# Output weights of a state space scan: four raw slots instead of two, and the across term scaled in the buffer of exp(cs)

## What is computed

```python
proj = hidden_states @ in_proj_w.T                 # gate, x/B/C, dt
hBC  = silu(conv(hBC) + conv_b)                    # 4 taps along time
A_cumsum = cumsum(-exp(A_log) * dt)                # "cs" of each head, within a chunk
Y_diag = einsum('bclsh,bcshp->bclhp', (C @ B.T) * exp(segment_sum(A)), x * dt)
Y_off  = einsum('bclhn,bchpn->bclhp', C, states) * exp(A_cumsum)[..., None]
y = Y_diag + Y_off + D * x
y = y * rsqrt(mean(y**2) + EPS) * norm_w
out = (y * silu(gate)) @ out_proj_w.T
```

## Time and profile before

| | us |
|---|---|
| median of 3 runs | 1904.71 |
| lowest, highest | 1900.41, 1908.31 |
| the profiled execution | 1903.86 |
| its span, first to last instruction | 1901.8 |

### The profile page before, as it was taken

How to read it: one execution, slowest core, us unless ns; L and a number is a source line. 1 busy time by engine, 2 the same in 40 slices (tenths; PEclk the granted TensorE clock), 3 DMA queues, 4 the chain that set the end, 5 groups by cost and what they waited for, 6 DMA issues and landing times. The chain is left out here.

```text
span 1901.8 us, 28929 instructions
## 1 busy us (share of the span) xinstructions
PE 1717.6 (90%) x9420; PEld 1395.2 (73%) x9420; DVE 1209.1 (64%) x1848; ACT 1264.8 (67%) x2162; POOL 738.2 (39%) x785
## 2 busy tenths in 40 slices
PE   5997739999999998999899989998999899999839
PEld 4876527787878787878787878787878787878627
DVE  4665555666666676657665766666766575767763
ACT  3331214986788778867786778677867786788711
POOL 2553012353345434543453345344434344444530
PEclk9998769999999999999999999999999999999969
DMA  4310114323232323332333232322332332232221
GB/s 149 105 62 1 61 58 121 100 85 107 78 102 88 105 84 102 94 93 84 98 91 100 80 99 86 102 79 92 101 96 77 98 98 87 85 100 80 67 70 44
DMA packets 99607, 166.93 MB, mean 88 GB/s; under 512 B 11729, under 2 KB 50129, under 8 KB 98033
## 3 DMA queue, kind: packets, MB, share of 16 engines
q1 hardware_dynamic: 99440, 164.84, 27.3%
HBM read 158.51 MB, written 6.29 MB: 87 GB/s over the span
## 5 line engine op out<-in xcount | busy, mean ns | idle before, releaser
L217 PE MATMUL bank<-xh,w_h 128*128 128x512 f32 x1152 | 463.7, 403 | 12.1 <-SPq L1083 11.3
L218 PE MATMUL bank<-xl,w_h 128*128 128x512 f32 x1152 | 451.2, 392 | 5.3 <-issue 5.3
L219 PE MATMUL bank<-xh,w_l 128*128 128x512 f32 x1152 | 451.5, 392 | 0.0
L1186 POOL TENSOR_TENSOR m_z_l<-m_zg,m_z_h 128x512 fp32r<-128x512 f32 x128 | 189.2, 1478 | 561.5 <-ACT m_z_h L1288 561.5
L1240 ACT ACTIVATE m_mt<-m_mt,m_unit 128x128 f32<-128x128 f32 x1024 | 312.1, 390 | 0.0
L1165 POOL TENSOR_TENSOR w_l<-w_raw,w_h 128x512 fp32r<-128x512 f32 x142 | 184.4, 1298 | 300.3 <-ACT w_h L1207 300.3
L1319 DVE TENSOR_TENSOR acc<-acc,bank 128x512 f32<-128x512 f32 x128 | 87.9, 687 | 301.9 <-PE bank L219 286.1
L217 PEld LDWEIGHTS bank<-xh,w_h 128*128 128x128 f32 x1152 | 217.5, 189 | 65.9 <-SPq L1083 11.5
L217 PE MATMUL bank<-m_wo_h,m_z_h 128*128 128x512 f32 x512 | 211.3, 413 | 55.0 <-DVE m_wo_l L1337 50.0
L1309 DVE SCALAR_TENSOR_TENSOR m_xc<-bank,m_par_conv,m_xc 128x1020 f32<-128x1020 f32 (+2 forms) x192 | 244.6, 1274 | 21.2 <-ACT m_xc L1219 16.6
L219 PEld LDWEIGHTS bank<-xh,w_l 128*128 128x128 f32 x1152 | 217.1, 188 | 52.7 <-issue 6.3
(11 more groups left out here) (238 smaller groups left out, 2804.7 us busy)
## 6 DMA issues: line engine op xcount, KB each, us to landing
m_mt<-ncs_rows SPq DMA_DIRECT2D x128, 512.0 KB, 3.9
w_raw<-w_in SPq DMA_DIRECT2D x144, 256.0 KB, 3.2
m_e<-ecs_rows SPq DMA_DIRECT2D x128, 128.0 KB, 3.5
m_wo_raw<-w_out_in SPq DMA_DIRECT2D x64, 256.0 KB, 2.7
a_wo_raw<-wo_in SPq DMA_DIRECT2D x8, 1024.0 KB, 4.7
x<-x_in SPq DMA_DIRECT2D x8, 256.0 KB, 4.6
a_wq_raw<-wq_in SPq DMA_DIRECT2D x8, 256.0 KB, 3.4
e_wb_raw<-f_base SPq DMA_DIRECT2D x2, 1024.0 KB, 7.9
```

The source lines that it names most:

```text
L217: nc.tensor.matmul(out, ah, bh, start=first, stop=False)
L218: nc.tensor.matmul(out, ah, bl, start=False, stop=False)
L219: return nc.tensor.matmul(out, al, bh, start=False, stop=last)
L1186: nc.gpsimd.tensor_tensor(z_l[:, s % 2, :, :], zg[:], f(z_h[:, s % 2, :, :]), ALU.subtract).then_inc(zl_ready, 1)
```

## The change

- WO_BUFS goes from 2 to CT = 4: each of a half's four tiles has its own raw slot.
- SP no longer loads tiles 2 and 3 of the present half in step t = 1. In t = 2 it loads all four of the next half, each after the low part that frees its slot. At the start four tiles are loaded ahead, not two.
- ScalarE, step t = 1: first the eviction and `w_high` of the step, then the four high parts, then `decay(s+2)`.
- VectorE, step t = 1: the four low parts in one row, behind `times_dt` and ahead of off, y and zg.
- The buffer `off` goes. The across term is written over the slot of `e` it was scaled with, and y adds that. SP's reload of the slot waits for `y_ready` of the step instead of `off_ready`.

```diff
-W_BUFS, WO_BUFS, ROW_BUFS = 3, 2, 4
+W_BUFS, WO_BUFS, ROW_BUFS = 3, CT, 4
...
-        off = sb("off", [P, CT, P])
...
                 def step(g, s, kind):
                     half, t = divmod(s, NT)
-                    if own(kind) and t == 1:
+                    if own(kind) and t == 2 and (half == 0 or kind != "last"):
                         for k in range(WO_BUFS):
                             sp.wait_ge(wo_split, wo_at(g, half, k))
-                            load_wo(g, half, k + WO_BUFS)
-                    if own(kind) and t == 2 and (half == 0 or kind != "last"):
-                        for k in range(WO_BUFS):
-                            sp.wait_ge(wo_split, wo_at(g, half, k + WO_BUFS))
                             load_wo(g + half, 1 - half, k)
...
                     if s % 2 == 1 and own(kind) and ahead(kind, s + 4):
-                        sp.wait_ge(off_ready, pair(g, s))
+                        sp.wait_ge(y_ready, at(g, s))
                         load_e(g, s + 4)
...
                     half, t = divmod(s, NT)
-                    if own(kind) and t == 1:
-                        for k in range(WO_BUFS):
-                            wo_high(g, half, k)
                     for m in EARLY[s]:
                         if has_tile(kind, m):
                             evict(g, m)
                             if has_tile(kind, m + 2):
                                 w_high(g, m + 2)
+                    if own(kind) and t == 1:
+                        for k in range(CT):
+                            wo_high(g, half, k)
                     if ahead(kind, s + 2):
                         decay(g, s + 2)
...
-                    if own(kind) and t == 1:
-                        for k in range(WO_BUFS, CT):
-                            wo_high(g, half, k)
...
                     if own(kind) and t == 1:
-                        for k in range(WO_BUFS):
+                        for k in range(CT):
                             wo_low(g, half, k)
...
-                            nc.vector.tensor_tensor(off[:], bank[:, 5, :].rearrange("p (c l) -> p c l", c=CT),
-                                                    e[:, s // 2 % 2, :, :], ALU.mult).then_inc(off_ready, 1)
+                            off = e[:, s // 2 % 2, :, :]
+                            nc.vector.tensor_tensor(off, bank[:, 5, :].rearrange("p (c l) -> p c l", c=CT), off,
+                                                    ALU.mult).then_inc(off_ready, 1)
...
-                            last = nc.vector.tensor_tensor(y[:], y[:], off[:], ALU.add)
+                            last = nc.vector.tensor_tensor(y[:], y[:], off, ALU.add)
...
-                        if t == 1:
-                            for k in range(WO_BUFS, CT):
-                                wo_low(g, half, k)
```

## The result

| | before | changed |
|---|---|---|
| median of the runs | 1904.32 us (4 runs) | 1828.84 us (4 runs) |
| lowest, highest | 1900.41, 1908.31 | 1827.55, 1829.94 |
| the profiled execution, its span | 1903.86, 1901.8 | 1827.55, 1825.8 |
| mean granted clock of TensorE | 0.954 | 0.966 |

The ratio is 0.9601, 95% interval 0.9581 to 0.9620. Forecast were 1833 us, range 1826 to 1860.

What follows compares the result with a forecast made beforehand. The prediction took TensorE's matmuls to bound the kernel. Terms of 44.6 + 23.6 + 3.0 = 71.2 us off the profiled 1903.86 gave 1832.7, and 0.85 to the median gave 1833 us, range 1826 to 1860.

Steps and rivals of the forecast that it cites:

- 15 waits on the lows: Step 1 of the 15 half groups with a projection: TensorE's wait ahead of add_up goes entirely, 44.6 us.
- clock behind them: TensorE's lowered clock in the 12 us after those waits returns to full: 23.6 us, bounds 0 and 25.2.
- last half of the last group: Step 9, no projection as cover: wait falls from 5.45 to some 2.3 us, gain 3.0 us, bounds 0 and 7.0.
- Highs in one row: ACT, step 1: eviction and w_high fit its idle time, then four highs end at 919.9, ahead of the decay.
- Lows in one row: DVE, step 1: four lows end at about 921.3, TensorE asks at 925.09; cover 3.8 us, so the wait goes.
- rival A: DVE's row of lows is stretched, 15 us given back: 1848 us, or 1872 with the cold clock too; chance 0.12.
- Slots and loads: Two more slots, SP's loads moved to step 2, seven steps ahead of use: cost 0.
- off in the buffer of exp(cs): Same instruction with another destination, slot reload some 2 us later under 44 us of cover: cost 0.
- B: Rival: TensorE's cold stretches stay or come elsewhere, 1856 us; chance 0.11.
- C: Rival: another wait stood behind the low parts' wait all the time, so no gain, 1904 us; chance 0.05.
- D: Rival: four highs ahead of the decay delay decay, mask and diag two steps later; slower, about 1924 us; chance 0.02.

Runs made afterwards that it cites:

- e1: The kernel before with four raw slots and the changed kernel's loads, highs and lows in their old places; 1906.86 us, ratio 1.0006.
- e2: The kernel before with four slots and the four highs in one row behind eviction and w_high, lows still split; 1834.95 us, ratio 0.9637.
- e3: The kernel before with four slots and the four lows in one row ahead of off, y and zg, highs still split; 1903.74 us, ratio 0.9989.
- e6: The changed kernel with the four highs ahead of the eviction and w_high instead of behind them; 1829.50 us, ratio 0.9598 to the kernel before.
- e5: The kernel before with twelve unused matmuls on TensorE ahead of the wait for the lows in add_up; 1877.24 us, ratio 0.9859.
- e4: The kernel before with only the across term scaled in the slot of exp(cs), no buffer off, reload waiting for y_ready; 1902.07 us, ratio 0.9978.
- c: The changed kernel itself, run once more as a yardstick; 1828.25 us, ratio 0.9602 to the kernel before.
- e8: The changed kernel with unused matmuls in TensorE's other long waits, 30 of them at the scan's start; 1815.76 us, ratio 0.9529 to the kernel before.

## Why the prediction was right

The gain of the profiled execution is 1903.86 - 1827.55 = 76.3 us; the forecast was 71.2.

| term | forecast | measured |
|---|---|---|
| 15 waits on the lows | 44.6 | 47.0 |
| clock behind them | 23.6 | 23.6 |
| last half of the last group | 3.0 | 2.9 |
| the last `add_up`, its clock | 0 | -1.6 |
| idle time at the loop's turns | 0 | 3.4 |
| ahead of the scan | 0 | 0.9 |
| sum | 71.2 | 76.2 |

*Highs in one row* was right with its numbers, in step 1 of group 3: ACT without idle time, four highs in 2.55 us. e1, e2 and e3 show that this is the step that carries the gain, and e6 that the eviction's new place does not.

*Lows in one row*: the row takes 3.3 us and not 3.0, since POOL's w_l, as rival A feared, now runs beside the first of them; the cover was 3.3 us, not 3.8, and held. That TensorE keeps what it wins held as well: 2.76 us for `add_up`, and no wait anywhere in steps 2 to 8. The term was sized a little too small. An idle time is counted to the end of the last matmul, but matmuls overlap: the next would have started at 924.93, not 925.09. The delay is 3.25 us where the row says 3.09, and 15 x 0.16 = 2.4 us is the difference.

*The clock* was right, in mechanism (e5) and size. That it came out to the tenth is luck: by the same windows the same fourteen waits cost 25.0 us in e1, 23.5 in e3 and 21.4 in e4.

*The last half*: forecast were a wait of 2.3 us and 3.0 us of gain; 2.43 and 2.9 came (from VectorE's first sum into acc in that half, 1762.46 and 1687.87, to the end of TensorE's last wait for z_l, 1813.31 and 1735.81: 50.85 us before, 47.94 after). The prediction put that wait down to the order alone; in the kernel before ACT also waited 0.36 and 0.41 us for the two late loads there (e1). The last wait is 2.51 us in both traces, but from its end to VectorE's last sum it took 1740.45 - 1735.81 = 4.64 us now and 3.06 before. This -1.6 is the execution's and not the change's: c, the same program, took 1743.06 - 1739.99 = 3.07.

*Slots and loads, off in the buffer of exp(cs)*: cost 0, as e1 and e4 show.

*The loop's turns* were not in the sum. Their idle time fell from 10.9 to 7.5 us; that is luck as far as these runs show. So are the 0.9 us ahead of the scan: c, the same program, comes to the scan's first projection 2.3 us later than the changed kernel's trace (282.61 and 280.30).

Of the rivals, A was present as a stretch of 0.6 us inside the cover (3.32 us for the row; 2.73 in e6, where w_l stands elsewhere). B is refuted by the 1.00 over the changed kernel's scan, and e5 shows the cause. C falls by the result, D by the result and by e6, where the decay ends 2.6 us later than in the changed kernel and costs nothing.

## What to carry to other kernels

When one engine is nearly always busy, look at its few long waits, follow the chain back from the instruction that ends each, and ask on every engine of that chain what stands ahead of it without need: here it was eight decay rows and a table load ahead of two short casts, and, but for 0.8 us in the last half, neither a load nor VectorE. Price such a wait twice where TensorE is the bound: by the delay from start to start, and by the granted clock of the microseconds behind it. If the wait can't be removed, a few matmuls whose result is not used gave the second price back here (e5), but they cost time themselves where they outlast the wait.

## What was not expected of the hardware

- The same waits do not always lower the clock. Of fourteen waits of 3.08 to 3.19 us in the kernel before, three were followed by 1.00; 2.2 and 0.8 us ahead of group 0 were followed by 1.00 in e8 and by 0.70 in all other traces; 2.43 us in the last half by 0.86 in the changed kernel's trace and by 1.00 in c, the same program. So the sum over many waits can be forecast to some 2 us (21.4 to 25.0 in four traces), a single one can't.
- A hardware loop cost TensorE 1.2 to 2.4 us at each of its five turns in the changed kernel, 9.4 in all, and 0.2 to 0.6 in e8 with the same loop of TensorE's instructions, 2.1 in all, by the lengths of the groups (none where it was written out).
- A filling that is longer than its wait costs at first: 8.4 us of matmuls into 1.7 us of wait made the next tiles 3.0 us late. Here the full clock behind it paid that back.
